# A transformer layer with two-way routed experts on one core: q and k split by GpSimd, logits computed in attention's last steps, the shared expert in units of two tiles

## The chip, the cores and the metric

The kernel runs on one core of a Trainium2 chip. The metric is the device time of one execution in microseconds (us). The engines of a core are TensorE (PE, with its weight loads PEld), VectorE (DVE), ScalarE (ACT), GpSimd (POOL) and SyncE (SP), which issues most of the DMAs. Each executes its own queue in order; they meet at semaphores.

## The reference, cut to what matters

```python
x = x + attn(layernorm(x))          # 16 sequences of 512 tokens, C = 256, 16 heads of 16, causal
x = x + ffn(layernorm(x))
# attn: q, k, v = split(x @ W_attn + b); rotary on q, k by head index;
#       softmax(q k^T / 4, causal) v; @ W_proj + b_proj
# ffn(x), 8192 tokens, 8 experts, two of them for each token:
probs = softmax(layernorm(x) @ gate_w.T);  top 2, normalised
swiglu(x, wg, wu, wd) = (silu(x @ wg) * (x @ wu)) @ wd      # 256 -> 512 -> 256
out = swiglu(x, shared) + sum over the two experts of weight * swiglu(x, expert)
```

The result is float32. Most products are made of float16 pairs: each operand is a high part and the rest that the high part leaves (a low part), and a product is three matmuls, high x high, high x low and low x high (the helper `products`, L1617).

## The kernel before, in words

**Attention** runs over NB = 16 batches of 512 tokens. A batch is four groups (`g`) of four heads and a group has five steps (`s`), so 20 steps; each engine has a function `body` that walks over the same steps, and tables such as `QK = ((0, 4), (1, 4), (2, 4), (3, 1))` say in which step (g, s) a piece of work is done. In a step PE computes scores (L1677, L1697) into `pair_s`, DVE takes their maxima (`row_max`, L1167 to L1173), PE computes the shifted scores of an earlier group into `pair_t` (L1724), ACT takes exponentials (L886), POOL cuts them causally (`select`, L702) and PE multiplies them with the values (`mix`, L1750). Beside this the next batch is prepared: its layernorm, the transposes of xn (L1608), and the projections of q, k and v, which all go through one PSUM bank, `ps_q`. For each of the four blocks of q and k ACT writes the high part in float16 with the bias (`qk_high`, L863) and DVE the low part (`qk_low`, L1079), both from the bank; PE may use the bank again when `qk_low` is done (`qkl_done`). SP stores both parts in DRAM and loads them again in the layout of the score products (`store_qk`, `load_qk`), and brings the row of maxima into q's operand by four DMAs for each group (`load_shift`, L480). The batch before is finished at the same time: o is transposed (L1766), divided (L1185), transposed again (L1774), projected (L1785), added to the residual (L1196; POOL adds the bias to it in `X_BIAS` steps, L723), normalised (L1222) and split into a high part by ACT (L903) and a low part by DVE (L1229); SP stores the rows x1_d and xhl_d (L511, L512).

**The drain.** `body` is called twice more (batches NB and NB + 1) with nothing new to score: the last groups and the last batch's output pass through. The shared expert's weights are split there too (L953, L1267).

**The shared expert and the routing.** 64 tiles of 128 rows, one after another (`shared_blocks` calls `shared` for each engine; partly in hardware loops). PE for a tile: the hidden values of the tile before are transposed (L1901), gate and up are six matmuls of 512 columns each into one bank each, the rows of the next tile are transposed (L1876), the tile before gets its down product (L1617, 12 matmuls of 256 columns). ACT: the high part of the hidden values (L975) and silu (L968). DVE: low part (L1486), hidden values (L1495), the copy of the transposed rows (L1481) and the result (L1503). SP loads rows and residual rows, and stores the result (L553, L559, L590).

In the first eight tiles the logits of all 64 tiles are computed as well: SP loads rows by 512 KB (L566), for a pair of tiles PE makes eight transposes (L1851), DVE or ACT copies them (L1473, L962), and PE makes twelve small matmuls (L1617). After tiles 8 to 20 DVE has one stage of the routing each (`AFTER`: best two experts, weights, counts of tokens of each expert, the slot of each token). The weights of the eight experts are loaded one matrix of 512 KB for each tile from tile 10 on (`load_matrix`, L602; a load waits for the one before), DVE takes their maxima in a first pass (L1524), and ACT and DVE split them in a second pass (L989, L1535). POOL scatters the tokens' numbers into lists in DRAM (`scatter`, L782, two indirect DMAs for each of 64 tiles t). They are paced by the count of results:

```python
pool.wait_ge(S["y_out"], EXPERTS_AT + 5 * t // 8)
```

At the end SP loads the lists (L631), and POOL gathers rows by them (L801).

**The routed experts** work in units: 64 of two tiles and 8 of one, weights chosen by a register. The weights are the stationary operand (`hidden_half`, L1981), so the hidden values come out transposed and aren't transposed again; two PSUM banks for each of gate, up and down; hidden values in two halves. A unit of two tiles has 80 matmuls: 24 gate, 24 up, 8 transposes, 24 down. DVE writes hidden values (L1575) and low part (L1581), ACT silu, high part and result (L1010, L1018, L1027), POOL adds the results to the output by indirect DMA (L820).

## Time and profile before

| | us |
|---|---|
| median of three runs (lowest, highest) | 1855.26 (1852.66, 1862.44) |
| the profiled execution | 1851.92 |
| its span, first to last instruction | 1850.2 |
| PE busy in the span | 1632.0 (88%) |
| DVE | 1168.0 (63%) |
| ACT | 855.0 (46%) |
| POOL | 781.3 (42%) |

Busy time is an average over stages with different limits. An engine's matmuls overlap, so a busy PE isn't PE at its peak. The granted clock of TensorE (PEclk) is given as a share of 2.4 GHz and was 0.967 over the span. An instruction's idle time is that of its engine just before it, with what released it; "issue" is a wait for nothing that the profile shows, and "remote" one for a queue that it doesn't know.

### The profile page before, as it was taken

The numbers are of one execution on the slowest core, as the hardware profiler recorded it, in microseconds if no ns is written. First come the engines' busy times: TensorE is split into PE (matmuls) and PEld (weight loads), VectorE is DVE, ScalarE is ACT, GpSimd is POOL, SyncE is SP. The second block draws the span as 40 slices with busy tenths as digits, with TensorE's granted clock in tenths as the row PEclk, the third lists the DMA queues.
The fourth block names the chain that finished last, engine by engine and source line by source line (L and its number), as shares of the span: only waits on it lengthen the run. The fifth ranks groups of instructions, "written<-read, shape, count | busy, mean of one in ns | idle before, by whom it ended". The sixth has DMA issues, their size and how long they took to land.

```text
span 1850.2 us, 45151 instructions
## 1 busy us (share of the span) xinstructions
PE 1632.0 (88%) x15314; PEld 1126.2 (61%) x15315; DVE 1168.0 (63%) x2062; ACT 855.0 (46%) x1273; POOL 781.3 (42%) x1005
## 2 busy tenths in 40 slices
PE   2689999999999999766997887888999999999996
PEld 2345555555545555334764555557999999999985
DVE  5578888888888888853477555663444444444342
ACT  1266666666666666632332122443444444444442
POOL 1033333333333333423003545544666666666652
PEclk9699999999999999978999989899999999999999
DMA  2322333333333333214454422222443443434332
GB/s 59 107 85 85 108 106 107 104 105 104 104 104 104 104 106 93 79 43 157 141 174 140 147 84 69 65 74 49 67 68 60 65 62 63 65 60 64 63 61 24
DMA packets 162563, 163.34 MB, mean 88 GB/s; under 512 B 23537, under 2 KB 153073, under 8 KB 162418
## 3 DMA queue, kind: packets, MB, share of 16 engines
q1 hardware_dynamic: 132210, 125.65, 22.3%
q0 software_dynamic: 30208, 35.81, 12.4%
q8 instruction: 85, 1.39, 0.3%
q14 instruction: 60, 0.49, 0.1%
HBM read 100.82 MB, written 60.30 MB: 87 GB/s over the span
## 4 chain that ended last, share of the span: by engine, by line
PE 66%; DVE 15%; issue 7%; another core or an unknown queue 4%; ACT 4%; DMA 2%; SPq 1%; POOL 1%; DVEq 0%; ACTq 0%; POOLq 0%
PE bank L1617 21%; PE pair_s L1981 10%; PE pair_s L1617 6%; PE bank L1981 5%; PE pair_t L1981 5%; PE bank L1750 4%; PE pair_s L1677 4%; DVE mx L1167 3%; PE pair_t L1724 2%; PE pair_t L1970 2%; PE bank L1766 2%; ACT qkh L863 2%; DVE mx L1170 2%; PE pair_t L1901 1%
## 5 line engine op out<-in xcount | busy, mean ns | idle before, releaser
L886 ACT ACTIVATE prob<-pair_t 128x1024 f32<-128x1024 f32 x320 | 327.5, 1023 | 246.5 <-PE pair_t L1724 241.6
L702 POOL TENSOR_SCALAR_AFFINE_SELECT prob<-prob 128x256 f32<-128x256 f32 (+1 forms) x448 | 197.4, 455 | 468.6 <-ACT prob L886 465.3
L820 POOL DMA_INDIRECT out_x<-ysb,tok_rows x136 | 218.3, 1605 | 203.8 <-ACT ysb L1027 153.7
L782 POOL DMA_INDIRECT tok_d<-tok_w,dest_i x128 | 127.0, 992 | 228.9 <-issue 160.8
L1981 PE MATMUL pair_s<-xt,wbuf 128*128 128x256 f16 (+1 forms) x1728 | 196.0, 269 | 4.3 <-DVE xt L1566 3.3
L1575 DVE SCALAR_TENSOR_TENSOR early<-pair_s,h_s,sg 128x512 f32<-128x512 f32 (+1 forms) x72 | 51.9, 721 | 221.9 <-PE pair_s L1981 209.7
L1617 PE MATMUL bank<-wbuf,early 128*128 x1632 | 190.3, 273 | 0.9 <-ACT ysb L1027 0.8
L1617 PE MATMUL pair_s<-wsh,xt 128*128 128x512 f16 x768 | 189.1, 397 | 0.9 <-issue 0.9
L1750 PE MATMUL bank<-prob,v_op 128*32 128x512 f32 (+3 forms) x2048 | 180.4, 448 | 2.0 <-POOL prob L702 1.9
L1018 ACT CAST early<-early 128x512 f16<-128x512 f32 (+1 forms) x144 | 85.6, 595 | 204.0 <-DVE early L1575 201.2
L1981 PEld LDWEIGHTS pair_s<-xt,wbuf 128*128 x1728 | 164.3, 98 | 25.4 <-issue 4.9
L1167 DVE TENSOR_REDUCE mx<-pair_s 128x2 f32<-128x1024 f32 x128 | 156.2, 1220 | 23.4 <-PE pair_s L1697 22.9
L1617 PEld LDWEIGHTS bank<-wbuf,early 128*128 128x128 f16 x1632 | 156.2, 98 | 19.2 <-issue 1.3
L1677 PE MATMUL pair_s<-k_op,q_op 48*128 48x512 f16 (+3 forms) x1024 | 127.6, 307 | 41.4 <-DVE mx L1167 19.2
L801 POOL DMA_INDIRECT xrow<-xhl_d,tok_rows x136 | 137.0, 1007 | 57.6 <-issue 36.9
L1170 DVE TENSOR_REDUCE mx<-pair_s 128x2 f32<-128x768 f32 x128 | 122.1, 954 | 16.6 <-PE pair_s L1697 15.9
L1677 PEld LDWEIGHTS pair_s<-k_op,q_op 48*128 48x128 f16 x1024 | 34.7, 94 | 160.5 <-DVE mx L1167 84.9
L1617 PEld LDWEIGHTS pair_s<-wsh,xt 128*128 128x128 f16 x768 | 77.1, 102 | 84.0 <-issue 15.4
L1581 DVE TENSOR_TENSOR early<-early 128x512 f16<-128x512 f32 (+1 forms) x144 | 94.8, 658 | 50.3 <-ACT early L1018 47.0
L1724 PE MATMUL pair_t<-q_op,k_op 49*128 49x512 f16 (+3 forms) x1024 | 123.4, 298 | 1.7 <-ACT prob L886 1.7
L975 ACT CAST hth<-pair_t 128x512 f16<-128x512 f32 x64 | 37.5, 586 | 155.6 <-PE pair_t L1901 115.1
L1617 PE MATMUL bank<-wsh,hth 128*128 128x256 f16 x512 | 88.1, 274 | 23.3 <-DVE htl L1486 12.4
(260 smaller groups left out, 3083.8 us busy)
## 6 DMA issues: line engine op xcount, KB each, us to landing
q_op<-qk_d SPq DMA_DIRECT2D x192, 64.0 KB, 2.4
k_op<-qk_d SPq DMA_DIRECT2D x192, 64.0 KB, 2.4
x_in<-in_L_attn_x SPq DMA_DIRECT2D x16, 512.0 KB, 4.2
qk_d<-qkh SPq DMA_DIRECT2D x32, 256.0 KB, 2.3
qk_d<-qkl SPq DMA_DIRECT2D x32, 256.0 KB, 2.7
xres<-in_L_attn_x SPq DMA_DIRECT2D x16, 512.0 KB, 4.6
x_d<-x SPq DMA_DIRECT2D x32, 256.0 KB, 2.1
xhl_d<-xhl SPq DMA_DIRECT2D x32, 256.0 KB, 2.5
```

Source lines behind the costliest of these rows:

```text
L702: last = nc.gpsimd.affine_select(out=v, in_=v, compare_op=ALU.is_ge, fill=0.0, base=0, pattern=[[0, v.shape[1]], [1, P]], channel_multipli ...
L782: pool.indirect_dma_start(out=tok_d, out_offset=bass.IndirectOffsetOnAxis(ap=dest_i[:, t, k:k + 1], axis=0), in_=tok_w[:, t, k, :], in_off ...
L801: pool.indirect_dma_start(out=xrow[:, k % GATHERED], out_offset=None, in_=xhl_d, in_offset=bass.IndirectOffsetOnAxis(ap=tok_rows[:, k, 0:1 ...
L820: pool.indirect_dma_start(out=out, out_offset=bass.IndirectOffsetOnAxis(ap=tok_rows[:, k, 0:1], axis=0), in_=ysb[:, k % ROWS_AHEAD], in_of ...
L886: nc.scalar.activation(prob[:, half, u].rearrange("p a n -> p (a n)"), pair_t[:].rearrange("p a n -> p (a n)"), ACT.Exp, scale=exp_by).the ...
L1167: last = nc.vector.tensor_reduce(dst[:, 2 * u:2 * u + 2, 3], pair_s[:], AX_X, ALU.max)
L1170: nc.vector.tensor_reduce(dst[:, c:c + 2, 2], pair_s[:, :, 0:384], AX_X, ALU.max)
L1617: last = nc.tensor.matmul(out, a, m, start=(i == 0), stop=(i == n - 1))
L1677: nc.tensor.matmul(ps_s[a][:, lo:lo + P * (q + 1)], q_op[64 * a:64 * a + KR, par, pair, P * q:P * (q + 1)], k_op[64 * a:64 * a + KR, par, ...
L1724: last = nc.tensor.matmul(ps_t[a][:, lo:lo + n], k_op[rows, par, pair, P * k:P * (k + 1)], q_op[rows, par, pair, P * k:], start=start, sto ...
L1750: last = nc.tensor.matmul(ps_o[32 * h:32 * h + 32, P * k:], v_op[:, vpar, k, GH * gg + h, :], pr[:, unit, h % 2, lo:lo + n], start=(piece ...
L1981: last = nc.tensor.matmul(out[:, w * k:w * k + w], wbuf[:, a], xt2[:, par, x, 0:w], start=(i == 0), stop=(i == 3 * CC - 1))
```

## The change

1. **q and k.** ACT writes the projected rows with their bias as float32 into a new tile `qkf` of two halves (`qk_rows`). POOL makes the high part by a copy to float16 and the low part by a subtraction (`qk_high`, `qk_low`), each after the select of its step. PE's waits for the bank are for `qkf_done`, ACT's. The first batch stays as it was. `X_BIAS` steps are moved.
2. **Row of maxima.** `mx` is laid out so that two DMAs for each group are enough where there were four.
3. **Logits.** The 30 pairs of the first 15 batches are computed in the drain, one pair for each of its last 31 steps (`DRAIN`, `drain_slot`): transposes in step k, copy on DVE (even k) or ACT (odd k), logits in step k + 1. The last two pairs are done in unit 0 of the shared expert.
4. **Shared expert.** 32 unrolled units of two tiles, with the routed stage's functions (weights stationary, two banks each). ACT copies the transposed rows, DVE does the results. Rows and residual rows are loaded six and four tiles ahead.
5. **What lies beside.** Routing stages in units 1 to 6, two for each; three weight matrices loaded for each unit from unit 2 on; first pass three for each unit from 10, scales after 19, second pass two for each unit from 20. The two products for the ranks are made one after another in one bank.
6. **Scatters** start when unit 7's first up product is done and are paced by that count (`u_in`, two for each unit), three t for each unit.

The pieces below are, in order: constants and tables, SP in the drain, SP in the shared expert, POOL, DVE, and PE.

```diff
-BEFORE_MAX = 40
+BEFORE_MAX = 28
-    MROWS = 4 * 16
+    MROWS = 2 * 16
...
+        qkf = sb_a("qkf", [P, 2, T], F32)
-        mx = sb_a("mx", [P, 2, GH, NT], F32)
+        mx = sb_a("mx", [P, 2, 2, 2, NT], F32)
...
-        ps_gate, ps_up, ps_down = (bank[0], bank[2]), (bank[1], bank[5]), (bank[4], bank[6])
+        ps_gate, ps_up, ps_down = (bank[0], bank[2]), (bank[1], bank[7]), (bank[4], bank[6])
...
-        EXP_AT, RANKS_AT, EXPERTS_AT = 15, 16, 20
+        LOADS_AT, FIRST_AT, SCALE_AT, SECOND_AT = 2, 10, 19, 20
+        EXP_AT, TOTALS_AT, RANKS_AT, SCATTERS_AT = 4, 4, 5, 15
...
-        QK, QK_HIGH = ((0, 4), (1, 4), (2, 4), (3, 1)), ((1, 0), (2, 0), (3, 0), (3, 4))
-        QK_LOW = ((1, 0), (2, 0), (3, 0), (0, 1))
+        QK, QK_ROWS = ((0, 4), (1, 4), (2, 4), (3, 1)), ((1, 0), (2, 0), (3, 0), (3, 4))
+        QK_HIGH, QK_LOW = ((1, 1), (2, 1), (3, 1), (0, 0)), ((1, 2), (2, 2), (3, 3), (0, 1))
-        X_BIAS = ((1, 4), (3, 2), (3, 2), (3, 2))
+        X_BIAS = ((1, 4), (2, 0), (2, 3), (2, 4))
...
+        SH_UNITS = TILES // 2
+        DRAIN = [(NB, g, s) for g in range(NG) for s in range(UN)][9:] + [
+            (NB + 1, g, s) for g in range(NG) for s in range(UN)]
+        PAIRS = 2 * (NB - 1)
...
+            def logit_rows(q):
+                if q < 2:
+                    sp.wait_ge(S["xn_done"], NB)
+                    sp.wait_ge(S["stats_taken"], NB)
+                else:
+                    sp.wait_ge(S["lxT_in"], 2 * q - 2)
+                for j in range(2):
+                    sp.wait_ge(xhl_stored[j], 16 * (q + 1))
+                sp.dma_start(lrow[:, q % 2], xhl_d[4 * P * q:4 * P * (q + 1), :].rearrange("(t p) n -> p t n", p=P)
+                             ).then_inc(lrow_loaded[q % 2], 16)
...
+            for u in range(SH_UNITS):
+                if u == LOADS_AT:
+                    sp.wait_ge(S["lg_in"], TILES // 2)
+                for n in (2 * u, 2 * u + 1):
+                    if n + 6 < TILES:
+                        rows(n + 6)
+                    store(n)
+                    if n + ROWS_AHEAD < TILES:
+                        residual_rows(n + ROWS_AHEAD)
+                for e, k in expert_parts(u, LOADS_AT, 3):
+                    load_matrix(e, k)
+                if u == SH_UNITS - 2:
                     for k in range(3):
                         sp.wait_ge(scattered[k], 32 * len(range(k, TILES, 3)))
...
+            def qk_high(n, i):
+                pool.wait_ge(S["qkf_done"], 4 * n + i + 1)
+                if some(32 * n):
+                    pool.wait_ge(qk_stored[i // 2], 32 * n)
+                nc.gpsimd.tensor_copy(qkh[:, i, :], qkf[:, i % 2, :]).then_inc(S["qkh_done"], 1)
+            def qk_low(n, i):
+                pool.wait_ge(S["qkh_done"], 4 * (n - 1) + i + 1)
+                nc.gpsimd.tensor_tensor(qkl[:, i, :], qkf[:, i % 2, :], qkh[:, i, :], ALU.subtract
+                                        ).then_inc(S["qkl_done"], 1)
...
-                pool.wait_ge(S["y_out"], EXPERTS_AT + 5 * t // 8)
+                pool.wait_ge(S["u_in"], SCATTERS_AT + 2 * t // 3)
...
+            for u in range(SH_UNITS):
+                unit_hidden(u, 0, 2 * P, 1)
+                if u == 0:
+                    take_pair(PAIRS, xtl_end, ps_lx[2])
+                unit_low(u, u % 2, 0, 2 * P)
+                unit_hidden(u, 1, 2 * P, 1)
+                unit_low(u, u % 2, 1, 2 * P)
+                if u > 0:
+                    result(2 * u - 2)
+                    result(2 * u - 1)
+                for stage in AFTER.get(u, ()):
+                    stage()
+                for e, k in expert_parts(u, FIRST_AT, 3):
+                    first(e, k)
+                if u == SCALE_AT:
+                    dve.wait_ge(S["topped"], 2)
+                    scale_columns(dve, link, 0)
+                for e, k in expert_parts(u, SECOND_AT, 2):
+                    second(e, k)
...
-                    pe.wait_ge(S["qkl_done"], 4 * n + i)
+                    pe.wait_ge(S["qkf_done"], 4 * n + i)
...
+                        k = drain_slot(b, g, s)
+                        if k < PAIRS:
+                            transpose_pair(k, lrow[:, k // 2 % 2], lrow_loaded[k // 2 % 2], 16 * (k // 4) + 16,
+                                           ps_lx[k % 2])
+                        if 0 < k <= PAIRS:
+                            logits(k - 1, xtl)
...
+            for u in range(SH_UNITS):
+                unit_hidden(u, u % 2, 0, 2 * P, None)
+                if u == 0:
+                    for k in range(2):
+                        transpose_pair(PAIRS + k, lrow_end, lrow_loaded[2], 16, ps_lx[2 + k])
+                unit_hidden(u, u % 2, 1, 2 * P, None)
+                if u == 0:
+                    for k in range(2):
+                        logits(PAIRS + k, xtl_end)
+                if u < SH_UNITS - 1:
+                    shared_rows(u + 1)
+                if u > 0:
+                    unit_down(u - 1, 1 - u % 2, 2, 2 * u - 2, None)
```

## Rows read from the trace of the kernel before

**Rows 1.** Table by stage: stretch, its length, busy time of each engine (instructions), granted clock, DMA share, GB/s.

```profile
350.00:809.00 459.00, 417.15 (x4263) 223.42 (x4259) 394.61 (x729) 295.57 (x405) 173.89 (x351) 1.00 0.32 97
818.00:851.00 33.00, 12.66 (x40) 8.96 (x40) 15.30 (x39) 7.51 (x10) 7.03 (x19) 0.60 0.21 70
924.00:985.00 61.00, 56.04 (x374) 35.63 (x373) 49.63 (x107) 18.02 (x27) 0.00 (x0) 0.97 0.53 160
985.00:1247.00 262.00, 216.04 (x1394) 133.98 (x1392) 160.11 (x271) 79.95 (x111) 130.56 (x132) 0.95 0.33 95
1262.00:1760.00 498.00, 498.00 (x4782) 448.40 (x4781) 207.84 (x298) 206.05 (x358) 308.74 (x236) 1.00 0.39 62
```

**Rows 2.** Waits, 300 to 576 us (six batches): waiting instruction, releaser, us in total, times, longest.

```profile
PE bank L1617 <- DVE qkl L1079: 8.1, 12, 0.7
...
PE bank L1608 <- DVE qkl L1079: 3.5, 6, 0.6
```

**Rows 3.** Groups by form, 300 to 576 us: operation, count | busy us, mean ns | idle before.

```profile
L702 POOL TENSOR_SCALAR_AFFINE_SELECT prob<-prob 128x256 f32<-128x256 f32 x144 | 59.0, 426 | 115.1 <-ACT prob L886 113.4 <-DMA xres<-in_L_attn_x 1.7
...
L1079 DVE SCALAR_TENSOR_TENSOR qkl<-bank,bcol,qkh 128x512 f16<-128x512 f32 x24 | 17.9, 746 | 11.3 <-ACT qkh L863 11.3
...
L723 POOL TENSOR_TENSOR xres<-xres,bpb 128x256 f32<-128x256 f32 x24 | 17.0, 729 | 0.1
...
L702 POOL TENSOR_SCALAR_AFFINE_SELECT prob<-prob 128x512 f32<-128x512 f32 x24 | 15.2, 634 | 51.7 <-ACT prob L886 51.7
...
L1229 DVE SCALAR_TENSOR_TENSOR xhl<-xf,xhl 128x512 f16<-128x512 f32 x12 | 10.2, 854 | 0.0
```

**Rows 4.** Groups of the drain, 818 to 851 us.

```profile
L1229 DVE SCALAR_TENSOR_TENSOR xhl<-xf,xhl 128x512 f16<-128x512 f32 x4 | 2.8, 690 | 1.4 <-ACT xhl L903 1.4
```

**Rows 5.** Timeline, drain and first logits: start, us, engine, line, operation [idle before <-releaser].

```profile
818.62 1.11 PE L1766 MATMUL bank<-ident,o_t 128*128 128x128 f32 x4 [0.71 <-ACT o_t L927]
...
851.13 0.58 PE L1876 MATMUL pair_t<-ident_h,xrow 128*128 128x128 f16 x4 [12.36 <-DMA xrow<-xhl_d]
...
858.50 0.61 PE L1851 MATMUL bank<-ident_h,wbuf 128*128 128x128 f16 x8
...
858.95 0.45 PE L1617 MATMUL bank<-gate_hl,wbuf 128*128 128x8 f16 x12
...
860.12 1.01 ACT L962 COPY wbuf<-bank 128x1024 f16<-128x1024 f16 x1 [1.87 <-PE bank L1851]
```

**Rows 6.** DMA issues of the page and of SP: size of one, median us to landing.

```profile
x_in<-in_L_attn_x SPq DMA_DIRECT2D x16, 512.0 KB, 4.2
...
wbuf<-xhl_d SPq DMA_DIRECT2D x16, 512.0 KB, 4.9
...
tok_rows<-tok_d SPq DMA_DIRECT2D x1, 136.0 KB, 2.4
```

**Rows 7.** Timeline, end of the shared expert.

```profile
1239.92 0.37 SPq L631 DMA_DIRECT2D tok_rows<-tok_d  x1
...
1247.14 0.39 PE L1970 MATMUL pair_t<-ident_h,xrow 128*128 128x128 f16 x4
```

**Rows 8.** Groups by form on VectorE, 924 to 1250 us.

```profile
L1495 DVE SCALAR_TENSOR_TENSOR hb<-pair_s,h_s,sg 128x512 f32<-128x512 f32 x55 | 41.1, 748 | 59.5 <-remote 24.0 <-ACT sg L968 14.5 <-PE pair_s L1617 12.6
L1486 DVE TENSOR_TENSOR htl<-pair_t,hth 128x512 f16<-128x512 f32 x56 | 38.5, 688 | 13.2 <-issue 5.9 <-ACT hth L975 3.6 <-DVE run L1527 3.4
L1524 DVE TENSOR_REDUCE top<-wbuf 128x1 f32 x24 | 29.0, 1208 | 0.0
L1503 DVE SCALAR_TENSOR_TENSOR ysb<-bank,y_s,x1t 128x256 f32<-128x256 f32 x56 | 27.0, 482 | 37.2 <-PE bank L1617 34.5 <-remote 1.5 <-issue 1.2
```

**Rows 9.** Timeline beside scatters, 1154 to 1157 us.

```profile
1154.54 0.96 POOL L782 DMA_INDIRECT tok_d<-tok_w,dest_i  x1 [0.31 <-issue]
1156.47 0.75 DVE L1495 SCALAR_TENSOR_TENSOR hb<-pair_s,h_s,sg 128x512 f32<-128x512 f32 x1 [6.53 <-remote]
...
1157.28 1.12 PE L1901 MATMUL pair_t<-ident,hb 128*128 128x128 f32 x4 [5.80 <-DVE hb L1495]
```

More of the change, by code:

```diff
@@ L715, in body @@
                             select(G - 2, s + 2 * UN - LAG, g % 2)
+                        for i in range(4):
+                            for at, half in ((QK_HIGH[i], qk_high), (QK_LOW[i], qk_low)):
+                                if (g, s) == at and at < QK[i] and cur and prev:
+                                    half(b, i)
+                                elif (g, s) == at and at >= QK[i] and nxt:
+                                    half(b + 1, i)
                         if prev:
@@ L1275, in body @@
                     for s in range(UN):
-                        for i in range(4):
-                            if cur and prev and (g, s) == QK_LOW[i] and QK_LOW[i] < QK[i]:
-                                qk_low(b, i)
                         if cur:
@@ L1284, in body @@
                                     xn_low(b + 1, c)
-                            for i in range(4):
-                                if (g, s) == QK_LOW[i] and QK_LOW[i] >= QK[i]:
-                                    qk_low(b + 1, i)
                             for j in range(2):
@@ L1507, in shared @@
-            def shared(n, par, half, prev, with_logits):
-                if with_logits:
-                    take_pair(4 * n)
-                if prev:
-                    low(n - 1)
-                hidden(n, par, 1)
-                if with_logits:
-                    take_pair(4 * n + 2)
-                if not isinstance(n, int) or n < TILES - 1:
-                    take_rows(n + 1, 1 - par)
-                if prev:
-                    result(n - 1, 1 - par, half - 1 if par == 0 else half)
@@ L1550, in beside @@
-            def beside(n):
-                if n in AFTER:
-                    AFTER[n]()
-            shared_blocks(dve, shared, beside, first, second, middle, link, 12)
-            low(N_SH - 1)
-            result(N_SH - 1, (N_SH - 1) % 2, (N_SH - 1) // 2)
+            AFTER = {1: (route_logits, lambda: largest(0, lg)), 2: (lambda: one_hot(0), lambda: largest(1, lg2)),
+                     3: (lambda: one_hot(1), choose), 4: (count, count_blocks), 5: (weigh, rows_in_order),
+                     6: (place, experts_of_units)}
@@ L1558, in _ @@
+            result(TILES - 2)
+            result(TILES - 1)
             dve.wait_ge(S["rows_in"], 16)
@@ L2014, in routed @@
                     pe.reg_load(offset[1 - par], unit_off[0:1, bass.ds(u + 1, 1)])
-                    unit_rows(u + 1, first + n, after, *slot_of(slot, turn, n))
+                    unit_rows(u + (SH_UNITS + 1), row_gathered, [place_of(slot, turn, n + t) for t in range(after)])
                 if before:
-                    unit_down(u - 1, 1 - par, before, first - before, at(offset_down))
+                    unit_down(u + (SH_UNITS - 1), 1 - par, before, first + (N_SH - before), at(offset_down))
```

637 lines of the change are left out of this document (251 added, 386 removed).

## The prediction, made before the change was run

> **What bounds the kernel now.** I read the page first, then the table by stage, the groups and waits of six batches of attention, the timeline of the drain and of the shared expert, and the DMA issues. The kernel is three stages behind one another. Attention has PE at 91% and DVE at 86% [rows 1]: neither is full, they hand one another single buffers. In the 276 us of [rows 2, 3] there are 24 `qk_low`, four a batch, so six batches of 46 us. What PE waits for there is mostly the release of the one bank of projections by DVE's `qk_low`: 8.1 and 3.5 us, 1.9 us a batch [rows 2]. The drain is a chain with PE busy 12.7 of 33 us and the granted clock at 0.60 [rows 1], between its two levels of 1.2 and 2.4 GHz. The routed stage has PE at 100% [rows 1] and is touched only by new counts; nothing moves there. The shared expert is the stage that can pay: of its last 262 us PE is busy 216 [rows 1], since one tile's gate, hidden values and down product have a single buffer each, and since GpSimd scatters beside them. Its first eight tiles carry the logits.
>
> **The change part by part**, against the profiled execution (1851.92 us, span 1850.2). The median of the runs shown is 1855.26, 3.3 us more, inside their spread.
>
> *Attention, q and k.* Fifteen batches are projected in the loop. DVE loses four `qk_low` of 0.75 us a batch [rows 3], 3.0 us, and with them ACT's result is all that PE waits for. ACT keeps four instructions of the same size. GpSimd gains four copies and four subtractions of 128x512 a batch. No row shows such a copy. Lower bound: the affine select of 128x512, 0.63 us; upper: a two-input operation, 0.73 us for 256 columns, so 1.46 for 512 [rows 3]. I take 0.7 (a copy has one input, as the select) and 1.46, so 8.6 us a batch on an engine that is busy 17.4 of 46 (173.9 of 459 us [rows 1]). They stand behind the selects of their step; a step is a twentieth of a batch, 2.3 us, with one or two selects of 0.43 [rows 3], so select and subtraction just fit (2.3), and `mix`, which waits for the select of the step before, is not delayed. The store of q and k comes some 2 us later and its loads are due two steps after that. Two row DMAs for each group in place of four cost nothing and give nothing, since PE does not wait for the row now. Gain: the 1.9 us of waits [rows 2], and 0.1 from earlier maxima: 2.0 x 15 = 30 us. Bounds: 2.9 a batch would be no PE idle at all, 43 us; at the other end GpSimd runs late, a loss of 20 (0.2 us in each of 15 x 8 places, doubled where PE hands it on to DVE).
> DVE's `low` of the residual has two operands in SBUF. It takes 0.85 us in attention [rows 3] and 0.69 in the drain, where GpSimd is mostly idle [rows 4]: something is already shared. The Trainium skill (SBUF — State Buffer, Who interferes with whom) says that a VectorE instruction with two SBUF inputs and a GpSimd instruction that reads SBUF block one another for a whole instruction. By that rule the trace agrees, and the change, which gives GpSimd eight more reading instructions a batch, speaks against itself here; the result is rival 2.
>
> *The drain with 30 pairs of logits.* A pair is eight transposes (0.61 us), twelve small matmuls (0.45) and one copy (up to 1.01) [rows 5]. The rows come by loads of 512 KB with 4.9 us to landing [rows 6], two buffers, one load for two pairs, each issued when the buffer's last pair is transposed. Two batches so need 4.9 + 0.61 + 0.45 + 0.61 = 6.6 us for four pairs, 1.65 us a slot. There are 31 slots from the first transpose of o to the end; these take 851.1 - 818.6 = 32.5 us now [rows 5]. Paced by the loads they take 51; with part of the old chain in series (PE, SP's stores and DVE's copies are in order, one step behind the other) I take 58. Cost +26 us. Bounds: +10 if the pairs fill the waits, +50 if all is in series.
>
> *The shared expert.* It ran on PE from 851.1 to 1247.1 [rows 5, 7], 396 us. The new unit of two tiles has the routed unit's instructions, 80 matmuls. Routed: 4782 matmuls in 498 us are 59.8 units, 8.33 us each, PE at 100% [rows 1]. So 32 x 8.33 = 266 us, 3 to the first gate, and 2 for the last two pairs of logits. On top come four terms:
> (a) Expert weights. They were loaded one for each tile, now three in SP's step of a unit, and each waits for the one before. A 512 KB load takes 4.2 us to land [rows 6], so three take 12.6 us against PE's 8.33, over the eight units from 2 on. SP issues the x rows, three units ahead, behind them. From the first gate: SP's step of unit 2 waits for that unit's results, out at 4 x 8.33 + 0.7 = 34, then loads at 35, 39 and 43; the next step's rows go out at 45 and land at 48 (3 us; 2.4 for 136 KB, 4.2 for 512 [rows 6]). PE wants them at 5 x 8.33 + 5.6 = 47. So 1 us late, and 4.3 more for each of seven further steps: 31 us. Bounds: 0 (loads that land within 2.8 us) to 45.
> (b) Routing on DVE. In 924 to 985 DVE is busy 49.6 us [rows 1], of which about 28 are twelve tiles' own work; the routing is 22, and about 4 more follow: 26 us in six units, each of which needs 2 x (0.75 + 0.69 + 0.48) = 3.8 itself [rows 8]. That is 8.1 us a unit, nearly full. The three longest steps would hold PE some 7 us, but they fall where (a) holds it anyway: 0.
> (c) First and second pass over expert weights. Three maxima of 1.21 us a unit [rows 8] and their small partners make 4.8, and with 3.8 the sum is 8.6 against 8.33: 3 us over eight units.
> (d) Scatters. Beside GpSimd's uninterrupted issue PE's signals come late: DVE started 6.53 us after it was free, released by nothing that the profile can name, and PE then stood 5.80 us, behind an issue every 0.96 + 0.31 = 1.27 us [rows 9]. PE's idle time in 985 to 1247 is 46 us for the 64 pairs of scatters that all fall there [rows 1], 0.7 us a pair. The new pace is three pairs a unit: 6 x 1.27 us = 7.6 us of 8.33, nearly without pause. The unit has about 1.2 us of slack between its row transposes and the next gate, so I expect 2 us lost in each of the 18 units that do not already wait for (a): 36 us. Bounds: 0 (the second banks absorb it) to 70.
> Sum: 3 + 266 + 2 + 31 + 0 + 3 + 36 = 341 us, 55 less than now. `take_rows` moves from DVE to ACT: ACT has then about 3.7 us of 8.33, and with two second passes under 6: 0. Unrolled bodies: 0, the routed stage shows PE full with both kinds.
>
> *Into the routed stage.* The list of rows was loaded at 1239.9 and the first gathered tile transposed at 1247.1, 7.2 us later [rows 7], hidden behind one and a half tiles of other work. Now SP loads it behind unit 30's stores, when only the last down product (2.6 us) is left. 7.2 - 2.6 + some issue: +6 us. Bounds 0 to 9.
>
> **Sum**: -30 + 26 - 55 + 6 = -53 us; 1851.9 - 53 = 1799. With the median 3 us above this execution, I say 1800.
>
> **Rivals.**
> 1. *No late loads, and the unit absorbs the scatters.* For it: PE, DVE and ACT have two banks of each product now, which the old tile had not. Against: x rows have to pass through SP behind three serial loads. Saves 31 of (a) and 25 of (d): 1744.
> 2. *GpSimd and DVE collide in attention.* For it: 0.85 against 0.69 us [rows 3, 4]. DVE has six instructions a batch there that could be hit; if each waits out one subtraction, 6 x 1.4 = 8.4 us return to DVE where 3.0 left, and the gain of attention is gone: 1830. Against: DVE is not full.
> 3. *The drain in series*: the pairs cost 50 in place of 26: 1824. For it: SP's loads stand behind stores that wait for DVE's last step.
> 4. *Slower: held signals in the scatter stretch.* If GpSimd's nearly unbroken issue holds PE in each of 22 units as long as the 5.80 us of [rows 9], that is 128 us in place of 36: 1892. It decides above a loss of some 4 us a unit: 53 / 22 = 2.4 more than the 1.6 in my sum. Against: in the routed stage GpSimd issues indirect DMAs 62% of the time and PE stands at 100% [rows 1]; the scatters wait for PE's own count, so held signals also slow them.
> 5. *The change does not do what it says*: it is plain in the code that `qk_low` leaves DVE and the logits leave the shared stage; that leaves no room for this.
>
> **How the numbers follow.** Forecast 0.46 (1775 to 1835), rival 1 0.18, rival 2 0.14, rival 3 0.13, rival 4 0.09. About 0.5%, 9 us, is what a measurement of this kernel can tell from no change. Faster by more than that: forecast, rivals 1 to 3 less what combinations of 2, 3 and a late load take away: 0.87. Within: 0.05, where 2 and 3 meet. Slower: 0.08, nearly all rival 4. The range takes in rival 1 and the combinations of 2 and 3 and leaves rival 4 and the best ends out: 1735 to 1850.
>
> **What would show it.** Attention: a batch of 44 us in place of 46, no wait on `qkl` by PE's projections; wrong if PE waits for `prob` by GpSimd or DVE's `low` is over 1.2 us. Drain: from its first transpose of o to the first row transpose some 58 us in place of 32.5. Shared: units of 8.3 us where nothing else happens, of about 12.6 while weights load with PE waiting for x rows, of 10 during the scatters with releasers that the profile cannot name. Routed: 8.33 a unit as now. The forecast falls if the units stay at 8.3 throughout (too slow a forecast) or if the scatter stretch takes over 12 us a unit.

## The result: 2.6% faster, and the profile after the change

The changed kernel takes 1809.5 us (median of 4 runs, 1807.3 to 1813.3) against 1858.9 us for the kernel before (4 runs, 1852.7 to 1864.2): ratio 0.974, 95% interval 0.971 to 0.976. The forecast was 1800. The profiled execution took 1808.7 us with a span of 1807.0, so 43.2 us less than the profiled one of before; the medians stand 49.4 apart, since the profiled execution of before (1851.92 us) was faster than each of its four runs and that of after lies among its own.

The table by stage of the changed kernel, in the columns of [rows 1]. The first and the last row answer to attention and the routed stage there, the second to the drain; between them the shared expert is cut where its behaviour changes.

```profile
350.00:750.00 400.00, 382.54 (x3940) 206.30 (x3938) 339.46 (x634) 269.46 (x374) 217.53 (x387) 1.00 0.35 107
791.00:847.00 56.00, 40.32 (x640) 36.76 (x640) 23.60 (x53) 20.48 (x24) 6.59 (x18) 0.71 0.52 164
893.00:990.00 97.00, 76.64 (x637) 63.15 (x637) 57.02 (x120) 31.13 (x45) 34.47 (x36) 0.91 0.64 192
991.00:1052.00 61.00, 51.15 (x480) 44.18 (x478) 45.21 (x71) 19.20 (x29) 21.44 (x23) 1.00 0.28 79
1052.00:1083.00 31.00, 13.85 (x83) 7.42 (x82) 4.15 (x7) 4.31 (x7) 20.33 (x21) 0.65 0.11 27
1083.00:1196.00 113.00, 105.35 (x952) 89.98 (x951) 72.79 (x107) 64.78 (x84) 53.57 (x50) 0.97 0.29 82
1220.00:1760.00 540.00, 538.09 (x5214) 483.80 (x5212) 224.77 (x328) 223.34 (x392) 333.46 (x254) 1.00 0.40 62
```

PE's share in attention rose from 91% to 96% and DVE's fell from 86% to 85%. The drain became long, and PE busier in it. In the shared expert there are three losses one behind another: 893 to 990 with PE at 79% and the DMA engines at 64%, a hole from 1052 to 1083 where PE is busy for 14 of 31 us and nobody else does much but GpSimd, and a smaller loss to the end. The lines that bound the stages, from the timeline of PE:

```profile
791.11 1.11 PE L1720 MATMUL bank<-ident,o_t 128*128 128x128 f32 x4 [0.71 <-ACT o_t L902]
...
847.37 1.08 PE L1849 MATMUL pair_t<-ident_h,xrow 128*128 128x128 f16 x8 [3.71 <-DMA xrow<-xhl_d]
...
1196.22 2.78 PE L1571 MATMUL bank<-wsh,early 128*128 128x256 f16 x24 [1.41 <-DVE ysb L1501]
1202.50 0.61 PE L1849 MATMUL pair_t<-ident_h,xrow 128*128 128x128 f16 x4 [3.50 <-DMA xrow<-xhl_d,tok_rows]
```

Set against [rows 5, 7] they give the four terms of the sum in this pair of executions. Attention ends 27.5 us earlier (the transposes of o: 791.11 for 818.62). The drain, from there to the first row transpose, takes 56.3 us in place of 32.5: +23.8. The shared expert, to the end of its last down product, takes 351.6 us (847.37 to 1196.22 + 2.78) in place of 396.0: -44.4 (before, the first gathered tile is transposed at 1247.14, as the last down product ends). What follows takes 608.0 us in place of 603.1 (1850.2 - 1247.14): +4.9. Sum -43.2. Forecast: -30, +26, -55, +6.

The waits of PE from 300 to 576 us, which answer to [rows 2]; the releases by `qkl` are gone, and one wait is new:

```profile
PE pair_t L1678 <- DMA q_op<-m_row: 3.2, 4, 1.4
```

The groups by form of the same stretch, which answer to [rows 3] (count | busy us, mean ns | idle before):

```profile
L644 POOL TENSOR_TENSOR qkl<-qkf,qkh 128x512 f16<-128x512 f32 x25 | 29.0, 1161 | 0.0
...
L639 POOL CAST qkh<-qkf 128x512 f16<-128x512 f32 x25 | 15.2, 609 | 0.0
...
L1206 DVE SCALAR_TENSOR_TENSOR xhl<-xf,xhl 128x512 f16<-128x512 f32 x13 | 8.8, 680 | 0.0
```

The copy took 0.61 us (0.7 taken), the subtraction 1.16 (1.46 taken). Counted by ACT's cast of the transposed x, one batch takes 43.6 us (547.75, 591.33, 634.88, 678.46) where 45.87 was the usual length before, but three between 282 and 548 us took 45.2, 44.3 and 44.8: there the row of maxima reached `q_op` late, the first line above.

**The loading stretch.** One unit of it in the timeline, first SP's queue, then PE, whose unit began at 893.43 and the next at 906.13:

```profile
899.98 0.38 SPq L555 DMA_DIRECT2D wbuf<-in_L_ffn_Wg  x1
...
904.31 0.38 SPq L555 DMA_DIRECT2D wbuf<-in_L_ffn_Wu  x1
...
907.89 0.37 SPq L555 DMA_DIRECT2D wbuf<-in_L_ffn_Wd  x1
908.31 0.51 SPq L536 DMA_DIRECT2D xrow<-xhl_d  x1
```

```profile
900.33 0.40 PE L1849 MATMUL pair_t<-ident_h,xrow 128*128 128x128 f16 x4 [1.50 <-DMA xrow<-xhl_d]
901.76 0.61 PE L1849 MATMUL pair_t<-ident_h,xrow 128*128 128x128 f16 x4 [1.03 <-DMA xrow<-xhl_d]
...
906.13 2.78 PE L1861 MATMUL pair_s<-xt,wsh 128*128 128x256 f16 x24
```

SP issues a load only when the one before has landed, 4.3 and 3.6 us apart, and the rows for a later unit come behind the third. Units 5 to 12 ran from 893.43 to 990.82: 97.4 us for eight, 12.2 each.

**The hole.** PE, ACT and GpSimd in the timeline around it:

```profile
1049.59 0.39 POOL L759 PARTITION_ALL_REDUCE top<-run  x1 [21.22 <-DVEq L1463]
1050.37 1.20 POOL L752 DMA_INDIRECT tok_d<-tok_w,dest_i  x1 [0.40 <-issue]
...
1052.59 2.79 PE L1861 MATMUL pair_s<-xt,wsh 128*128 128x256 f16 x24 [0.44 <-ACT xt L976]
...
1071.16 0.37 PE L1571 MATMUL bank<-wsh,early 128*128 128x256 f16 x1 [1.03 <-issue]
...
1077.55 0.96 POOL L752 DMA_INDIRECT tok_d<-tok_w,dest_i  x1 [0.30 <-issue]
...
1081.82 1.01 ACT L976 COPY xt<-pair_t 128x1024 f16<-128x1024 f16 x1 [16.33 <-remote]
...
1082.89 5.30 PE L1861 MATMUL pair_s<-xt,wsh 128*128 128x256 f16 x24 [6.40 <-ACT xt L976]
```

After 28 pairs of scatters GpSimd waits 21 us for DVE's last maximum, reduces it over the partitions, and then issues the 22 scatters it owes without a pause, 1050.4 to 1078.5. ACT's copy of rows that PE had transposed by 1059.3 starts at 1081.8, after 16.33 us of waiting for something the profile cannot name; the trace's record of semaphore updates has none for these transposes before 1081.06. PE's own matmuls come mostly one at a time, 0.7 to 1.4 us apart. The DMA engines are nearly idle (0.11 in the table). Unit 19 took 30.3 us.

### The profile page after: what moved, and what is told of

It is laid out like the page before. It is cut to its first block, busy times and chain, and to the rows that moved or that the text cites. A ratio compares the mean times of both kernels' runs of the same rounds, so it can differ in the third digit from the quotient of the medians.

```text
span 1807.0 us, 44792 instructions
## 1 busy us (share of the span) xinstructions
PE 1611.0 (89%) x15824; PEld 1177.5 (65%) x15827; DVE 1105.0 (61%) x1938; ACT 881.9 (49%) x1305; POOL 888.4 (49%) x1125
## 4 chain that ended last, share of the span: by engine, by line
PE 67%; DMA 8%; issue 7%; DVE 6%; SPq 4%; ACT 3%; POOL 2%; another core or an unknown queue 2%; DVEq 0%; POOLq 0%; ACTq 0%
PE bank L1571 19%; PE pair_s L1861 13%; PE bank L1704 7%; PE pair_t L1861 6%; PE bank L1861 6%; PE pair_s L1631 4%; PE pair_t L1678 3%; PE bank L1739 3%; PE pair_t L1849 2%; SPq L435 2%; DMA wbuf<-in_L_ffn_Wu 2%; ACT prob L861 2%; DMA qk_d<-qkl 1%; DMA x_in<-xhl_d 1%
## 5 line engine op out<-in xcount | busy, mean ns | idle before, releaser
L968 ACT CAST early<-early 128x512 f16<-128x512 f32 (+1 forms) x208 | 125.1, 602 | 298.7 <-DVE early L1484 244.7
L1484 DVE SCALAR_TENSOR_TENSOR early<-pair_s,h_s,sg 128x512 f32<-128x512 f32 (+1 forms) x104 | 75.9, 729 | 243.6 <-PE pair_s L1861 209.6
L1490 DVE TENSOR_TENSOR early<-early 128x512 f16<-128x512 f32 (+1 forms) x208 | 139.2, 669 | 119.7 <-ACT early L968 86.7
L960 ACT ACTIVATE sg<-pair_s,silu_s 128x512 f32<-128x512 f32 (+1 forms) x104 | 69.7, 670 | 120.9 <-PE pair_s L1861 100.2
L1861 PE MATMUL pair_s<-xt,wsh 128*128 128x256 f16 x768 | 94.3, 280 | 20.7 <-ACT xt L976 12.5
L1571 PE MATMUL bank<-wsh,early 128*128 128x256 f16 x768 | 101.0, 289 | 11.2 <-issue 9.7
L1004 ACT ACTIVATE ysb<-bank,row_w 128x256 f32<-128x256 f32 x136 | 64.1, 473 | 91.5 <-PE bank L1571 88.3
```

Of the source, the lines that this page charges most:

```text
L1490: nc.vector.tensor_tensor(htl2[:, par, 2 * hh:2 * hh + 2, 0:w], hb2[:, hh, 0:2 * w].rearrange("p (c n) -> p c n", c=2), hth2[:, par, 2 * h ...
L1571: last = nc.tensor.matmul(out, a, m, start=(i == 0), stop=(i == n - 1))
L1861: last = nc.tensor.matmul(out[:, w * k:w * k + w], stationary, xt2[:, par, x, 0:w], start=(i == 0), stop=(i == 3 * CC - 1))
```

## The experiments

The theory: three terms (late x rows behind serial loads; scatters that hold PE's signals, which is to say that the semaphore updates after PE's matmuls come late beside them; a full DVE) make up what the shared expert takes beyond 8.33 us a unit, and attention's gain is the release of one bank. Runs that were sent together ran on one chip, beside the kernel before. The four sets met four different chips, and these turned out to differ: the kernel before took 1790.9 us beside e1 to e4, 1849.7 beside e5 to e8, 1791.7 beside e9 and e11, 1791.6 beside e12 and e13. Units are counted from 0, by PE's first gate product of each.

**e1: the maximum behind 35 pairs of scatters.**

```diff
-BEFORE_MAX = 28
+BEFORE_MAX = 35
```

> The cross-partition maximum stands behind 35 pairs of scatters in place of 28, so GpSimd is not held 21 us for the last maxima and owes nothing after them. Theory (a burst of 22 scatters one behind another at 1050 to 1078 us holds PE's signals, and unit 19 takes 30.3 us for that reason): no burst, unit 19 near 10.4 us, time 18 to 20 us below the changed kernel, about 1790. Rival (those 30 us are DVE's scales and maxima, or instruction loading of the unrolled code): no change, within 3 us.

Measured: 1770.1 us, ratio 0.989 (0.986 to 0.991). The ratio is worse than that of the changed kernel, the time better; the kernel before is 68 us faster here too, so the chip lies behind both. Units 19 to 30 take 8.31 us each here: scatters hold nothing. What is left beside them is 9.69 us in units 14 to 17, here in the timeline of PE and DVE:

```profile
1001.13 2.79 PE L1861 MATMUL pair_s<-xt,wsh 128*128 128x256 f16 x24
...
1007.87 0.75 DVE L1484 SCALAR_TENSOR_TENSOR early<-pair_s,h_s,sg 128x512 f32<-128x512 f32 x1 [0.25 <-DVE run L1461]
1009.30 0.69 DVE L1490 TENSOR_TENSOR early<-early 128x512 f16<-128x512 f32 x1 [0.69 <-ACT early L968]
...
1010.82 2.79 PE L1861 MATMUL pair_s<-xt,wsh 128*128 128x256 f16 x24 [1.21 <-ACT xt L976]
```

DVE has the first pass over expert weights there, three maxima ahead of its line shown, and then stands 0.69 us while ACT casts. Units 14 to 18 take 48.8 us in place of 41.6: 7.2 us. Whether the burst makes the hole can't be told on this chip.

**e2: two loads a unit in place of three.**

```diff
-                for e, k in expert_parts(u, LOADS_AT, 3):
+                for e, k in expert_parts(u, LOADS_AT, 2):
                     load_matrix(e, k)
```

> Two matrices of expert weights loaded in each of SP's twelve steps 2 to 13, in place of three in eight steps. Theory (units 5 to 12 take 12.2 us because x rows pass SP behind three loads of 4.2 us, 30.8 us over eight units): two loads take 8.4 us of 8.33, x rows are hardly late, gain 20 to 28 us of which some 2 to 4 may be given back where loads now meet scatters, about 1785 to 1790. Rival (the rows are late because the DMA engines are full, whatever the order): the same bytes take as long, gain under 8 us.

Measured: 1750.6 us, ratio 0.976 (0.974 to 0.979), 19.6 us under e1 on the same chip; the changed kernel itself was not in this set. The run keeps the place of the maximum behind 28 pairs, so it has the same burst, and shows what it does on this chip, in the timeline and in the table by stage:

```profile
1033.98 0.39 POOL L759 PARTITION_ALL_REDUCE top<-run  x1 [20.51 <-DVEq L1463]
1034.77 1.20 POOL L752 DMA_INDIRECT tok_d<-tok_w,dest_i  x1 [0.40 <-issue]
...
1036.98 2.79 PE L1861 MATMUL pair_s<-xt,wsh 128*128 128x256 f16 x24 [0.64 <-ACT xt L976]
...
1045.30 2.78 PE L1861 MATMUL pair_s<-xt,wsh 128*128 128x256 f16 x24
```

```profile
1034.00:1071.00 37.00, 36.37 (x350) 32.47 (x348) 24.20 (x43) 21.86 (x30) 28.67 (x28) 1.00 0.31 88
```

The same 0.96 us scatters follow one another 1.26 us apart, and PE is busy for 36.4 of 37 us. The code and the 22 scatters are those of the hole; the chip is another.

**e3: the three loads of an expert at once.**

```diff
-                if 3 * e + k > 0:
-                    sp.wait_ge(S["w_exp"], 48 * e + 16 * k)
+                if k == 0 and e > 0:
+                    sp.wait_ge(S["w_exp"], 48 * e)
```

> The three loads of one expert are issued together, SP waits only for the expert before. Theory (the loss is the serial wait in SP, latency and not bandwidth): three loads land together in some 6 to 8 us and SP passes at once, units 5 to 12 return to some 8.5 to 9.5 us, gain 20 to 30 us. Rival (bandwidth): x rows queue behind 1.5 MB in the DMA queue, rows land as late as now, gain under 8 us.

Measured: 1744.6 us, ratio 0.975 (0.972 to 0.978), 25.6 us under e1. PE's waits in the loading stretch hold no x rows any more (the changed kernel had 15.4 us for them from 893 to 990), and SP passes three loads and the next rows within 2 us. Waits of 893 to 970 us, then SP's timeline:

```profile
PE pair_s L1861 <- ACT xt L976: 7.0, 3, 2.7
```

```profile
896.78 0.49 SPq L555 DMA_DIRECT2D wbuf<-in_L_ffn_Wg  x1
...
897.83 0.47 SPq L555 DMA_DIRECT2D wbuf<-in_L_ffn_Wd  x1
898.34 0.57 SPq L536 DMA_DIRECT2D xrow<-xhl_d  x1
```

So latency in series was the loss, not bandwidth. Units 5 to 12 take 77.3 us in place of 100.6 in e1. Three of them stay above 8.33: 10.34, 11.10 and 12.89, 9.4 us together. These are DVE's routing steps, which the late rows had covered.

**e4: half of the scatters taken out of the shared stage.** The second choice's 64 scatters are issued after its last unit.

```diff
-                for k in range(2):
+                for k in (1,) if late else (0,):
...
+            for t in range(TILES):
+                scatter(t, True)
```

> Only the first choice's scatter of each tile stays in the shared stage, the other 64 follow after its last unit (these add some 81 us between the stages, so only the shared stage is read, not the total). Theory (signals are held only while GpSimd issues four or more scatters without pause): runs of three with 4 us between them, units 13 to 18 and 20 to 30 near 8.4 us, against 10.3 and 9.5 now; the burst after the maximum is half as long and costs half of its 22 us. Rival (every scatter costs PE its 0.35 us, whatever the spacing): units lose half of what they lose now, about 9.3 and 8.9.

Measured: 1844.1 us in a single run, with units of 9.70 us in 14 to 17 and 8.31 from 19 on, as in e1. On a chip that holds no signals this tells nothing of spacing. It agrees with the 9.69 us units owing nothing to scatters: half as many leave them as they are.

**e5: the changed kernel again.** No edit.

> The changed kernel itself, as reference on this chip; the kernel before took 1858.9 us on one chip and 1790.9 on another, and in the runs e1 to e3 units beside scatters took 8.31 us, with a burst of 20 scatters as well. Theory (how much GpSimd's unbroken issue holds PE's signals differs from chip to chip): on a chip where the kernel before takes about 1791 the changed kernel takes some 1770, with unit 19 near 8.3 to 10 us; where it takes about 1859 it takes some 1809, with unit 19 near 30 us. Rival (the place of the maximum decides, also on this chip): unit 19 takes 30 us and the kernel some 1790 even where before takes 1791.

Measured: 1805.8 us against 1849.7, ratio 0.977 (0.973 to 0.980), unit 19 at 30.0 us. For these two it is on record that they ran on one chip, and the change brings 2.3% there. With the first pair of runs (it isn't known whether that was the same chip) the hole is there in two sets, and with e1 to e3 it is missing in one. The theory of the chip agrees on this side; its other side (about 1770 for the unchanged code of the changed kernel) was only come near, by e1.

**e6: q and k split by ACT and DVE as before.**

```diff
-                nc.scalar.activation(qkf[:, i % 2, :], src[:], ACT.Identity,
-                                     bias=bcol[:, i:i + 1]).then_inc(S["qkf_done"], 1)
+                nc.scalar.activation(qkh[:, i, :], src[:], ACT.Identity,
+                                     bias=bcol[:, i:i + 1]).then_inc(S["qkh_done"], 1)
...
+                nc.vector.scalar_tensor_tensor(out=qkl[:, i, :], in0=ps_q[:], scalar=bcol[:, i:i + 1],
+                                               in1=qkh[:, i, :], op0=ALU.add,
+                                               op1=ALU.subtract).then_inc(S["qkl_done"], 1)
```

GpSimd's copy and subtraction are left out, and PE waits for `qkl_done` where it waited for `qkf_done`.

> The changed kernel with q and k split as before: ACT writes the upper half from the bank, DVE the lower half from the same bank, and GpSimd does neither. Theory (the bank's release by DVE cost 2.3 us a batch, 1.9 of it seen as waits): batches of 45.9 us in place of 43.6, some 28 to 34 us slower than the changed kernel. Rival (the two row transfers in place of four and the earlier maxima bring the gain): within 8 us of the changed kernel.

Measured: 1833.2 us, ratio 0.993 (0.990 to 0.995), 27.4 us over e5. The waits of PE in 300 to 576 us are those of [rows 2] again:

```profile
PE bank L1564 <- DVE qkl L1043: 8.1, 12, 0.7
...
PE bank L1555 <- DVE qkl L1043: 3.4, 6, 0.6
```

PE's first transposes of o come at 819.42, where they came at 818.62 before and at 793.78 in e5. So within the spread the split is the whole of attention's gain; row transfers and maxima bring none. That spread isn't small: in the runs with the changed attention these transposes come between 786.0 and 794.0.

**e7: the drain's rows in loads of 256 KB.** Four buffers of two tiles in the place of two of four.

```diff
-                    sp.wait_ge(S["lxT_in"], 2 * q - 2)
+                    sp.wait_ge(S["lxT_in"], k - 3)
...
-                sp.dma_start(lrow[:, q % 2], xhl_d[4 * P * q:4 * P * (q + 1), :].rearrange("(t p) n -> p t n", p=P)
-                             ).then_inc(lrow_loaded[q % 2], 16)
+                sp.dma_start(lrow[:, k // 2 % 2, 2 * (k % 2):2 * (k % 2) + 2],
+                             xhl_d[2 * P * k:2 * P * (k + 1), :].rearrange("(t p) n -> p t n", p=P)
+                             ).then_inc(lrow_loaded[k % 4], 16)
```

> In the drain each pair of logit tiles is loaded by itself, 256 KB into one of four buffers, in place of 512 KB for two pairs into one of two. Theory (the last 14 pairs, 22 us, are paced by loads of 4.9 us for two buffers): about 1.2 us a pair in place of 1.65, gain 5 to 9 us. Rival (SP's order and the copies pace them): no gain, within 3 us.

Measured: 1795.4 us, ratio 0.970 (0.967 to 0.972), 10.3 us under e5. PE waited 8.5 us for the loads between 786 and 858 us in e5, and 2.2 us here:

```profile
PE pair_s L1806 <- DMA x_in<-xhl_d: 2.2, 2, 1.7
```

The first gate product moved from 851.0 to 840.0, but not all of this is the drain's. In the timelines of e5 and of e7, from the first transposes of o to the first row transposes:

```profile
793.78 0.66 PE L1720 MATMUL bank<-ident,o_t 128*128 128x128 f32 x4 [0.71 <-ACT o_t L902]
...
848.66 1.07 PE L1849 MATMUL pair_t<-ident_h,xrow 128*128 128x128 f16 x8 [3.65 <-DMA xrow<-xhl_d]
```

```profile
789.43 0.66 PE L1720 MATMUL bank<-ident,o_t 128*128 128x128 f32 x4 [0.71 <-ACT o_t L902]
...
837.71 1.01 PE L1849 MATMUL pair_t<-ident_h,xrow 128*128 128x128 f16 x8 [4.76 <-DMA xrow<-xhl_d]
```

The drain took 54.9 us and takes 48.3: 6.6 us, inside the 5 to 9 expected. The other 4.4 are an earlier end of attention, where nothing was edited. The loads paced the pairs.

**e8: all together.** Loads at once (e3), drain by pairs (e7), maximum behind 35 pairs (e1), and the maxima two a unit from unit 7:

```diff
-        LOADS_AT, FIRST_AT, SCALE_AT, SECOND_AT = 2, 10, 19, 20
+        LOADS_AT, FIRST_AT, SCALE_AT, SECOND_AT = 2, 7, 19, 20
...
-                for e, k in expert_parts(u, FIRST_AT, 3):
+                for e, k in expert_parts(u, FIRST_AT, 2):
```

> Loads of one expert issued together, the maxima of expert weights two a unit from unit 7 in place of three from unit 10, the cross-partition maximum behind 35 pairs of scatters, and the drain's loads by pairs. Theory: 25 us from the loads, 10 from the maxima (units of 9.69 us become 8.3), 7 from the drain, so some 42 us under the changed kernel where signals are not held, and some 60 where they are. Rival (DVE's step with routing and maxima is only moved): 30 us or less.

Measured: 1764.9 us, ratio 0.954 (0.951 to 0.957): 40.9 us under the changed kernel, where 60 were expected on such a chip. By the traces of e8 and e5 the drain paid 7.6 us, the loading units 5 to 12 paid 12.2 and units 19 and 20 paid 15.8; another 4.1 are an earlier end of attention. The loads were to pay 25: units 9 to 18 still took 9.7 to 10.9 us, so with scatters beside them neither the prompt rows nor the easing of DVE gives a unit of 8.31. In the burst, now 14 scatters with one short pause, unit 20 took 16.0 us where unit 19 had taken 30 (the table of that stretch, then GpSimd's timeline):

```profile
1033.00:1052.00 19.00, 14.07 (x113) 10.99 (x111) 6.76 (x18) 5.89 (x9) 13.45 (x15) 0.90 0.18 49
```

```profile
1032.74 0.38 POOL L759 PARTITION_ALL_REDUCE top<-run  x1 [6.08 <-DVEq L1463]
1033.46 1.20 POOL L752 DMA_INDIRECT tok_d<-tok_w,dest_i  x1 [0.34 <-issue]
...
1051.40 0.96 POOL L752 DMA_INDIRECT tok_d<-tok_w,dest_i  x1 [0.30 <-issue]
```

A shorter burst, a shorter hole: 22 scatters cost 22 us, these 14 cost 8. ACT's copy of the transposed rows, with which the next unit can start, comes within some 3 us of the burst's end in both (1081.8 for 1078.5, 1050.8 for 1052.4), though single signals get through before. And this settles a rival on a chip that holds signals: unit 19, with the code and DVE's scales of the hole, took 8.3 us in e8. The hole went with the burst, so neither the loading of that unit's code nor its work on DVE makes it.

**e9, e11 and e12: two tries for a chip that holds signals.** e9 is the kernel of e1. e11 and e12 are one kernel, in which each scatter waits for a signal of its own:

```diff
-                pool.wait_ge(S["u_in"], SCATTERS_AT + 2 * t // 3)
...
                 for k in range(2):
+                    u, event = SCATTERS_AT // 2 + (2 * t + k + 1) // 6, (2 * t + k + 1) % 6
+                    name, count = (("g_in", 2 * u + 1), ("u_in", 2 * u + 1), ("g_in", 2 * u + 2),
+                                   ("u_in", 2 * u + 2), ("xT_in", 2 * u + 4), ("yp_in", 2 * u - 1))[event]
+                    pool.wait_ge(S[name], count)
```

> The kernel of e1 once more, for a chip on which signals are held (the kernel before takes some 1850 to 1860 there; if it takes some 1790 here, nothing is to be learned beyond e1). Theory (a burst of 22 scatters costs unit 19 some 20 us): unit 19 near 10 to 12 us in place of 30, ratio to the kernel before 0.963 to 0.967 in place of 0.975. Rival (GpSimd owes the same scatters whatever the place of the maximum, or the loss is DVE's): ratio above 0.972.

> As e9, and each single scatter waits for one of six signals of a unit (gate, up, gate, up, rows, down product) in place of six scatters that follow one another at two signals; number and mean pace are the same. Theory A (a signal of PE passes when GpSimd stops issuing, so it is late by the length of the run of scatters): runs of one or two, units beside scatters lose 0.5 us in place of 1.5 to 2, some 15 us under e9. Theory B (each scatter costs PE its 0.7 us a pair, however it is spaced): within 4 us of e9. Either could be slower than e9 where late signals now also delay the scatters themselves.

> The kernel of e11 once more, for a chip on which signals are held (the kernel before at some 1850; at some 1790 nothing is to be learned beyond e11). Theory A (late by the length of an unbroken run): unit 19 near 10 us in place of 30, the other units beside scatters near 8.8 to 9.2 (10.1 where DVE takes maxima) in place of 9.5 to 10.4, ratio to the kernel before some 0.958. Theory B (each pair of scatters costs 0.7 us whatever the spacing): unit 19 near 10.5, the others as they were, ratio some 0.965. Rival (late signals delay the next scatter, scatters pile up at the end): the list of rows comes late and the ratio is above 0.97.

Measured: 1765.1 us, ratio 0.985 (0.984 to 0.987) for e9; 1766.5 us, ratio 0.987 (0.984 to 0.989) for e11; 1763.6 us, ratio 0.984 (0.981 to 0.987) for e12. All three met chips like that of e1, with units of 8.31 us beside the scatters. So what e9, e11 and e12 were expected to show on a chip that holds signals was not tried. They show that single pacing costs nothing measurable on the others (1.4 us, inside the spread), and leave open whether the spacing or the number of scatters counts where signals are held.

**e13: e8 with the maximum behind 38 pairs.** The edit is that of e1, to 38.

> The kernel of e8 with the maximum behind 38 pairs of scatters in place of 35; in e8 the maxima were there at 1032.7 us, GpSimd had stood 6 us and then issued 14 scatters in a row beside a unit of 16 us. Theory: where signals are held that unit takes 10 us and the ratio falls from 0.954 to some 0.950; where they are not, the kernel is 35 to 42 us under the 1765 to 1770 of e1, since loads (25 us), maxima (10) and drain (7) do not hang on that. Rival (the scales now come too late for unit 19's step): 2 to 5 us slower than e8 in that unit.

Measured: 1729.8 us, ratio 0.966 (0.964 to 0.968), on the chip of e12, 33.8 us under it, where 35 to 42 under e1's kernel were expected. The table of eleven units, and what came after them on DVE, in the timeline:

```profile
925.00:1016.00 91.00, 91.00 (x879) 82.08 (x877) 69.32 (x110) 37.54 (x55) 62.88 (x66) 1.00 0.51 152
```

```profile
1023.97 0.17 DVE L387 TENSOR_SCALAR top<-top 128x4 f32<-128x4 f32 x1 [6.93 <-POOL top L759]
```

PE is busy without a gap for 91 us beside 62.9 us of scatters: two maxima a unit fit. But at 38 the maximum is too late: DVE waits 6.93 us for it, and this unit and the next take 12.0 and 10.0 us, 5.4 lost. The rival had that right, in the two units after 19. e8 and e13 have the lowest ratios of the case; they met different chips, so which place of the maximum is better was not settled.

## Why the prediction was right, and which of its steps were off

The forecast case came in, 9 us slower than its number and inside its own range (1775 to 1835). Its terms came near one by one, but that of the scatters did so by luck.

*Attention, -30: measured -27.5 by the trace; e6 gives 27.4 by its time and 25.6 by its trace.* The bank's release was the whole gain, as said. A clean batch gains 2.3 us in place of 2.0, but some batches give 0.7 to 1.6 back. The step that failed is "two row DMAs ... cost nothing and give nothing, since PE does not wait for the row now": once PE no longer waits for the bank, a late row of maxima is the next wait, 3.2 us in six batches (in e6, with the same two DMAs, PE waits for the bank and not for the row). That SP's queue, where the row stands behind the later stores of q and k, makes it late is argued from the code and was not tried.

*Rival 2, the collision of GpSimd and DVE: it did not come.* DVE's `low` fell from 0.85 to 0.68 us. The 0.85 was a mean of two kinds: in the trace of before six of the twelve took 0.68, with GpSimd idle, and six took 1.03, each beginning during one of GpSimd's additions of the bias. The change had moved these additions (`X_BIAS`), and after it every `low` takes 0.68. The timelines of before and after, each where one meets GpSimd:

```profile
333.70 2.10 POOL L723 TENSOR_TENSOR xres<-xres,bpb 128x256 f32<-128x256 f32 x3
...
335.33 1.03 DVE L1229 SCALAR_TENSOR_TENSOR xhl<-xf,xhl 128x512 f16<-128x512 f32 x1
335.75 0.87 POOL L702 TENSOR_SCALAR_AFFINE_SELECT prob<-prob 128x256 f32<-128x256 f32 x1
```

```profile
303.02 0.68 DVE L1206 SCALAR_TENSOR_TENSOR xhl<-xf,xhl 128x512 f16<-128x512 f32 x1
303.29 1.03 POOL L665 TENSOR_SCALAR_AFFINE_SELECT prob<-prob 128x256 f32<-128x256 f32 x2 [0.52 <-ACT prob L861]
```

Before, DVE's instruction started 0.47 us before the end of GpSimd's additions and took 0.35 us longer; a select that came 0.61 us before its end took 0.87 in place of 0.41. After, DVE was first, and the two selects, begun 0.41 us before its end, took 1.03 us for 0.77. The one that comes second pays, here between 0.6 and 0.8 of what the first still had to run. The Trainium skill (SBUF — State Buffer, Who interferes with whom) has a VectorE instruction with two SBUF inputs and a GpSimd instruction that reads SBUF contend for a port pair that is an exclusive lock. The trace agrees that the second is held, if for somewhat less than the first's whole rest. What the rival got wrong is how often they meet. It counted six instructions of DVE a batch; only `low`, two a batch, shows the stretch in these traces (the scaling of the residual takes 0.42 us before and 0.43 after), and GpSimd's new work is not there when `low` runs.

*The drain, +26: measured +23.8.* Right in size, and right that the loads pace it (e7). Rival 3, all in series, did not come.

*The shared expert, 341 us: measured 351.6.* By terms: the unit takes 8.31 us, so 266 stands. Its start, unit 0 and its end add 8.4 where 3 + 2 were put. (a) Late x rows, 31: units 5 to 12 took 97.4 us for 66.5, 30.9, and e3 shows serial latency as the cause. Scatters run beside the last of these units too, but add nothing there: e1, where they hold nothing, needs 100.6. (b) Routing, 0 because it is covered: 9.4 us appear as soon as (a) is gone (e3), where the forecast named 7. (c) Maxima, 3: measured 7.2 in e1. The step that failed is its sum for DVE, 8.6 us: it left out that DVE stands 0.69 us between the hidden values and their low part, twice a unit, while ACT casts. With that the sum would be 10.0; the unit takes 9.69. (d) Scatters, 2 us in each of 18 units, 36: about 39 measured, nearly the number, but by another course, and that is the luck. Units 13 to 18 took 61.8 us for 49.9, of which 7.2 are the maxima: 4.7. Units 20 to 30 took 103.9 for 91.4: 12.5. That is 1 us a unit, half of what was taken. How 13 to 18 divide between (c) and (d) is borrowed from e1's chip; in e8, with two maxima a unit, units 9 to 18 still lost 1.7 us each where e13 loses none from unit 9 to 19, so the two limits hide one another and scatters alone may cost more than 1 us there. The other 22 us are unit 19 alone. The prediction read the new pace of scatters from the code and did not follow GpSimd's queue past `wmax_done`, behind which 22 scatters gather. Rival 4, as much as 5.8 us held in each unit, did not come, but its mechanism was real, and in one unit stronger than it said.

*Into the routed stage, +6: measured +4.9.* PE waits 3.50 us for the first gathered rows after its last down product.

Rival 1 (no late loads, scatters absorbed) was half true of three chips: on those the unit did absorb the scatters (e1, e2, e9, e12), while the loads stayed late. So the forecast's term for scatters held because of the chip it was measured on, which nothing in the rows could tell; the changed kernel itself was not measured on such a chip.

What stays open: whether it is the chip (each was met in one set of runs, so chip and occasion can't be told apart), why signals are held in one set and not in another, and whether it is the unbroken run or the number of scatters that costs where it does.

## What to carry to other kernels

When a queue is paced by counts, follow it past every wait for something else: what it owes afterwards comes as a burst, and here 22 us of 39 lay in that. A serial chain of loads in the queue that also feeds the bound engine costs latency, not bandwidth; issuing the three together took 23 us off eight units. And compare variants on one chip: here chips differed by more (58 us at least) than the change brought.

## What the runs showed that was not expected

The same program runs 58 to 68 us apart on different chips: the kernel before took 1849.7 and 1858.9 us in two sets, 1790.9, 1791.7 and 1791.6 on three other chips. For the changed kernel much of such a difference can be placed: 39 us of held signals on one kind, none on the other, where e1, with its one edit, runs 36 us under e5. For the kernel before there is no trace from a chip where it takes 1791.

Where signals are held, PE itself slows: single matmuls of 0.27 to 0.38 us came 0.7 to 1.4 us apart, with the DMA engines at 0.11, and the granted clock of that stretch fell to a mean of 0.65, between the levels of 1.2 and 2.4 GHz, while PE stood. In the routed stage of that chip GpSimd is busy, nearly all of it with indirect DMAs, for 333 of 540 us and PE is busy for 538, so issuing alone doesn't do it. All that follows the shared expert took 606 to 608 us in the runs that hold signals and 601 to 602 in those that don't (e4 apart, whose late scatters stand there).
